# Four products with zeros a batch in place of eight, in the two attention stages with heads of 8 dimensions

## What is computed

```
q = xn @ Wq ; k = ctx @ Wk ; v = ctx @ Wv
p[h,s,t] = exp((q[s,h] . k[t,h] - max) * 8**-0.5)
o[s,h]   = sum_t p[h,s,t] v[t,h] / sum_t p[h,s,t]
x        = x + gate * (o @ Wo)
```

## Time and profile before

| | |
|---|---|
| median of 3 runs | 5703.66 us (5700.96 to 5715.34) |
| the profiled execution | 5709.04 us, its span 5707.3 us |
| mean granted clock of PE | 0.929 |
| PE busy | 4836.8 us (85%) |
| DVE busy | 3943.6 us (69%) |
| ACT busy | 2707.8 us (47%) |
| POOL busy | 2171.1 us (38%) |

### The profile page before, as it was taken

The page is one execution under the profiler, slowest core; times in us unless marked ns, Lnnn a source line. Parts: engine busy times, 40 slices in busy tenths (PEclk is TensorE's granted clock), DMA queues, the critical chain, the costliest instruction groups (busy, mean ns, idle before and its releaser), DMA issues. The chain is left out here.

```text
span 5707.3 us, 133493 instructions
## 1 busy us (share of the span) xinstructions
PE 4836.8 (85%) x41659; PEld 3572.5 (63%) x41659; DVE 3943.6 (69%) x9897; ACT 2707.8 (47%) x5454; POOL 2171.1 (38%) x3095
## 2 busy tenths in 40 slices
PE   7998988999933995099989989888998799998898
PEld 4665658888822663066656657766776577776554
DVE  5776857777755332277767758888886799897544
ACT  4665755555510332066645545555554455554344
POOL 5442001011146002655533347777776533333200
PEclk9998989999965998599999989999999899998878
DMA  1004100000021442100000000000000000000000
GB/s 39 8 5 204 51 13 6 5 5 5 5 68 57 136 138 92 46 8 6 4 13 1 0 10 0 0 0 0 0 0 6 8 2 2 2 2 5 1 13 17
DMA packets 108941, 140.24 MB, mean 25 GB/s; under 512 B 35832, under 2 KB 83256, under 8 KB 103996
## 3 DMA queue, kind: packets, MB, share of 16 engines
q1 hardware_dynamic: 100544, 120.88, 6.3%
q0 software_dynamic: 8192, 16.79, 1.0%
HBM read 47.44 MB, written 58.72 MB: 19 GB/s over the span
## 5 line engine op out<-in xcount | busy, mean ns | idle before, releaser
L2180 POOL TENSOR_TENSOR l3a_probs<-l3a_probs,l3a_later 128x512 f32<-128x512 f32 x256 | 320.6, 1281 | 4.9 <-DVE l3a_total L2368 4.9
L2166 POOL TENSOR_TENSOR l3a_keys<-l3a_kT,head 128x2048 f32<-128x2048 f32 x64 | 230.4, 3600 | 232.4 <-ACT l3a_kT L2293 232.4
L1595 POOL DMA_INDIRECT l1c_rows<-l_rows,l1f_slots x128 | 122.5, 957 | 443.0 <-PEq L1587 402.4
L170 POOL TENSOR_TENSOR l1x_ve<-l1x_mv,eps 128x1 f32<-128x1 f32 x64 | 12.1, 190 | 659.9 <-DVE l1x_mv L162 659.9
L2228 PE MATMUL l3a_scores<-l3a_keys,l3a_qT 128*128 128x512 f32 x512 | 255.2, 601 | 4.2 <-POOL l3a_keys L2166 4.2
L1666 POOL TENSOR_TENSOR l2f_hid<-l2f_prod,l2f_route 128x512 f32<-128x512 f32 x128 | 152.2, 1194 | 256.6 <-DVE l2f_prod L1813 246.7
L298 PE MATMUL l3a_po<-l3a_vals,l3a_probsT 128*128 128x32 f32 x2048 | 248.0, 270 | 0.2
L254 ACT ACTIVATE l3a_probs<-l3a_probs 128x512 f32<-128x512 f32 x256 | 161.6, 631 | 182.1 <-DVE l3a_probs L245 177.0
L298 PEld LDWEIGHTS l3a_po<-l3a_vals,l3a_probsT 128*128 128x128 f32 x2048 | 246.9, 192 | 0.7 <-ACT l3a_probsT L279 0.4
L1514 PE MATMUL l1e_h<-l1e_xhi,l1f_parts 128*128 128x512 f16 x640 | 205.0, 382 | 9.6 <-DVE l1e_gated L1572 8.1
L2166 POOL TENSOR_TENSOR l3c_keys<-l3c_kT,head 128x1232 f32<-128x1232 f32 x64 | 144.0, 2250 | 156.7 <-ACT l3c_kT L2293 156.7
(11 more groups left out here) (581 smaller groups left out, 17124.0 us busy)
## 6 DMA issues: line engine op xcount, KB each, us to landing
l_rows<-l0f_zeros SPq DMA_DIRECT2D x34, 1024.0 KB, 26.2
l1f_parts<-l1f_split SPq DMA_DIRECT2D x40, 512.0 KB, 3.6
l1e_x_in<-l_rows SPq DMA_DIRECT2D x40, 256.0 KB, 2.8
l1f_down<-l1f_w SPq DMA_DIRECT2D x40, 256.0 KB, 2.3
l_rows<-l1e_y_out SPq DMA_DIRECT2D x40, 256.0 KB, 2.7
l1f_w<-in_L_W SPq DMA_DIRECT2D x16, 256.0 KB, 3.3
out_x<-x_res SPq DMA_DIRECT2D x16, 256.0 KB, 2.0
x_res<-in_x SPq DMA_DIRECT2D x1, 3840.0 KB, 12.5
```

The source lines that it names most:

```text
L2166: pool.tensor_tensor(keys[it.par][:, :, :, :], kT[it.par][:, :, :].unsqueeze(2).to_broadcast([P, J, G4, T]), g.head32[:, :].unsqueeze(1).u ...
L2180: pool.tensor_tensor(v, v, later[:, :].unsqueeze(1).to_broadcast([P, 4, T]), ALU.mult).then_inc(s_masked, 1)
```

## The change

The condition under which a product with zeros is emitted becomes another. Before it stood behind every piece of units 0 and 1, eight a batch; now it stands behind pieces 0, 2, 4 and 6, four a batch. The product itself, the order of all else, and all waits are as before. The other engines' orders are the same as before.

```diff
@@ -805,7 +805,7 @@
                             v = vv[it.par][i][0:rows, 10 * (j % 2) + c, 0:z - a + 1, :].rearrange("p i e -> p (i e)")
                             last = pe.matmul(cols, pp[u][0:rows, at(k)], v, start=(c == 0 and m == 0), stop=(c == 9 and m == 2),
                                              skip_group_check=True)
-                        if u < 2:
+                        if c < 8 and c % 2 == 0:
 
                             pe.matmul(po[:, HEADS * E1:BANK], blank[:, 0:P], blank[:, HEADS * E1:BANK], start=False, stop=False,
                                       skip_group_check=True)
```

## The result

| | before | after |
|---|---|---|
| median of 5 runs each, same chip | 5713.59 us (5700.96 to 5716.03) | 5673.57 us (5670.44 to 5683.65) |
| ratio, 95% interval | | 0.9939 (0.9928 to 0.9950) |
| the profiled execution | 5709.04 us, span 5707.3 | 5683.65 us, span 5681.9 |
| mean granted clock of PE | 0.929 | 0.923 |

The changed kernel is faster by 0.61% (0.50 to 0.72), which is some 35 us of 5713.59; the two medians as they stand are 40 us apart. The forecast of 5656 against a median of 5703.66 is a ratio of 0.9916, and its range goes from 0.9885 to 0.9962: the result lies inside, 13 us short of the point. The profiled execution of after is the slowest of its five, so its own gain is less, 25 us.

A forecast was written before the change was run, and what follows sets the result against it. PE was taken to bound the two stages, with waits for DVE in places: 512 products at 0.155 give 79 us, of which 48 reach the end (1.50 a group, 32 groups), so 5703.66 becomes 5656, range 5638 to 5682.

The forecast's parts named there:

- The price of a product: On PE in l0x and l2x: each product removed frees 0.155 us, 512 of them 79 us.
- rival D: No change, 5704 us: products hide the weight loads behind them, or DVE's chain holds the whole group; chance 0.05.
- How much reaches the end, slot by slot: Per group of four batches: slots 1, 2, 0, 3 gain 0.40, 0.48, 0.62, 0; 1.50 us, 48 us over 32 groups.
- Rivals B: All 79 us comes through, since DVE and ACT move up with PE: 5625 us, group 25.9 us; chance 0.10.
- C: DVE binds in slot 0 as well, losing 0.62 us more a group: 5676 us, L806 waiting there; chance 0.12.
- A: The main sum: PE gives 79 us, waits for DVE keep 31; 5656 us, 5644 to 5668 with bounds; chance 0.62.
- The new waits: L806 waits some 0.2 us for p_lo in slots 1 and 2; the turn of o waits up to 0.6 longer.
- The hand-over from DVE to PE: From p_lo to unit 1's weight load: shortest 0.06 us; if not below 0.15, the sum is 42 us.
- The clock: PE's granted clock in both stages stays at 1.00, chance nearly 9 in 10; if not, 2.7 us a slot.
- the prediction's own sign: In the profile after, PEclk inside the two stages below 1.00 would show the forecast wrong.
- The rows that were taken for a clock that holds: Stretches at 1.00 without such products: 2601.7 to 2606.0, and 3600 to 3800 in another stage.
- The rival E: Some of 128 slots fall to the lower clock: 18 eat the 48 us, 43 give 5772, all about 6000; chance 0.11.

The follow-up runs named there:

- e3: Changed kernel with all eight products back in the first eight batches of each stage; 5671.67 us, ratio 0.9933 to the kernel before.
- e1: Changed kernel with its four products a batch behind pieces 0 to 3, all in unit 0; 5664.21 us, ratio 0.9932 to the kernel before.
- e4: Changed kernel with no products at all; 5874.90 us, ratio 1.0293 to the kernel before.
- e5: Changed kernel with eight products in the one batch of each group weighed in slot 3; 5683.38 us, ratio 0.9918 to the kernel before.
- e6: Changed kernel with eight products in slot 3's batch and in each stage's first eight batches; 5679.76 us, ratio 0.9917 to the kernel before.

## Why the prediction was right, and by how much not

- **The price of a product, 0.155 us**: held. The product at 2592.47 is followed by the next matmul at 2592.62. That the loads behind a product hide it, the first half of rival D, would have made the gain nothing, and is refuted by the result. The Trainium skill ("TensorE: Matmul & The Clock Gate", section "Back-to-back issue gap") is no witness for that half, though the prediction took it for one: its 81 ns are for matmuls of 128 columns, and these have 18 or 27. For up to 64 columns the same section has a floor of about 25 ns, given for matmuls by themselves, and the 25 ns of the earlier trace rows, loads included, agree with that.
- **How much reaches the end, slot by slot**: held. Read between the first weights of unit 1, where the forecast's terms can be separated: from slot 0 to slot 1, 6.94 us fell to 6.53 (2607.32 - 2628.77 + 28.39, and 2593.17 - 2613.48 + 26.84), a gain of 0.41 against 0.31 + 0.09; from slot 1 to slot 2, 6.91 fell to 6.42, a gain of 0.49 against 0.31 + 0.17; from slot 2 over slot 3 to the turn of o in slot 0, 9.56 fell to 9.24 (2623.79 - 2614.23, and 2608.83 - 2599.59), a gain of 0.32 against 0.31 for slot 2's unit 1 and nothing for slot 3; from there to slot 0's unit 1, 4.98 fell to 4.65, a gain of 0.33 against 0.31 (before's times from the earlier trace rows). The group of 28.39 became 26.84; the forecast was 26.9. Rivals B (25.9) and C (a wait of L806 in slot 0) are refuted; D too. By the time alone A and C could not be told apart: 0.9939 of 5703.66 is 5669, just beyond A's own bounds (5644 to 5668) and nearer to C's 5676 than to A's 5656. The group and the waits decide for A.
- **The new waits**: held. L806 waits 0.21 to 0.29 in slots 1 and 2 (said: 0.2); slot 3 has 0.21 as well, which the forecast did not name; it costs nothing, since the turn of o behind it waits for DVE in any case. The hand-over from DVE to PE, 0.06 by the forecast and 0.15 by its other bound, is 0.05 in slot 1: p_lo starts at 2592.43 and takes 0.69, and PE loads at 2593.17. The turn of o waits 0.45 longer (said: up to 0.6). DVE is busy 303.10 of 386.70 us, 78% as said.
- **The clock**: this is the term that was mis-sized. By the prediction's own sign (PEclk inside the stages below 1.00) this part of it was wrong: 0.95 in l2x, and the stages end 13.6 and 10.9 us earlier, not 24. It was taken as a matter of holding or not holding in the steady state, with nothing for the rest. Measured, it has two costs. At the start of the stages the rise comes later, 14.6 us in both together, and it did so in both profiled executions. Inside, short falls cost 6.8 us in the profiled execution. Without both, the two stages would have gained 24.5 + 14.6 + 6.8 = 45.9 us, near the 48. With 48 us less 14.6 the forecast would be 5670, a ratio of 0.9941, and the result is 0.9939; less 6.8 as well it is 26.6 us, and the two profiled executions are 25.4 apart. How many falls the other executions had is not on record. That the result lies in the range in spite of the clock is in part luck: the range reached to 5682 to take in C, not a clock that costs 21 us. The row for it was there: the start of l2x at 0.50 was read only for what a slot costs at that level, not for what ends that level. As e3 shows, the full eight end it sooner, and the change takes half of them away just there; e1 shows that where the other half stands matters as well. The rows that were taken for a clock that holds, above all the 4.3 us with no product at 1.00, were no sign of it: e4 has such stretches of 10.2 us at 1.00 too, between longer ones at 0.50.

The rival E priced the right mechanism, at the wrong place: it asked how many of 128 slots would fall, and the answer is six stretches of 3.4 or 6.8 us, next to 22 and 30 us more at the lower level at the stages' starts.

**What stays open.** What the chip asks of PE to raise or keep the clock was not settled. e4 shows that the turns, scores and small products alone do not hold it, and e5 that four more products at one place are enough for no fall to be seen; neither says what is counted. Nor is it known why four products behind unit 0 let the clock rise early and four spread over both units don't. In l0x the record of the clock begins at 48.9 us before and 71.4 after, so the low level ahead of that is read from durations alone. Why e6 gains less by its median than its second groups promise is not explained.

## What to carry to other kernels

Price filler work by where it stands: ahead of a wait that is due anyway it is free, behind it every piece costs its full time, so four products behind unit 0 make a group of l0x 1.9 us shorter than eight do, and 1.0 us shorter than four behind unit 1. But such a place can cost the clock: look for pauses of the matmuls as well, and put products into them. When such work exists to hold the clock, look at the start of the stage apart from its steady state, since the clock has yet to rise there, and both the number of products and their place decide how long it stays low. And forecast the clock as a sum of stretches with a place each, not as held or lost.

## What the runs showed of the hardware that was not expected

PE busy time says little on the clock: e4 had PE busy 406.35 of 420 us at a mean clock of 0.62, and in after the clock fell at 2638.2 behind 3.4 us with PE busy 2.93. The longest pause of the matmuls in the 10 us ahead of that fall is this wait for o; timeline of after:

```profile
2635.67 0.14 PEld L816 LDWEIGHTS l2x_turned<-ident,l2x_o 128*128 128x128 f32 x1 [0.71 <-DVE l2x_o L987]
2635.67 0.33 PE L816 MATMUL l2x_turned<-ident,l2x_o 128*128 128x128 f32 x1 [0.39 <-DVE l2x_o L987]
```

Weight loads paused for 0.71 us and matmuls for 0.39. The Trainium skill ("TensorE: Matmul & The Clock Gate", section "HAM oscillation — how this bites in real kernels") puts such falls down to long pauses between bursts, in its example while the engine waits for DMA. The traces here show falls of the same kind with no long pause: what went ahead of this one were 40 matmuls of 16 or 24 columns, twelve of scores, a few fp32 ones and one short wait, and of the twelve falls in the two profiles of the changed kernel none has a longer pause of the matmuls than 0.39 us in the 10 us ahead of it.

Products of zeros with zeros, whose result nobody reads, do count for the clock: they are all that differs between e4 and the changed kernel, and the clock in l2x goes from 0.61 to 0.99 in the steady part. Section "Part 4: PE-mode transpose" of the same page says that turns through the array don't count in the same way. e4 agrees so far as a stage of turns, scores and small products does not hold the clock; no run here takes the turns apart from the rest.
